# One denominator group per iteration, added up by VectorE in four pieces, with the gates kept in DRAM during attention

## The chip, the cores and the metric

The kernel runs on one core of a Trainium2 chip. The time is device microseconds of one execution; the median of three runs is the figure that is compared.

## What is computed

A transformer block with conditioning, in fp32, on x of 2 x 2048 x 512, 16 heads of 32. Cut to what matters:

```
c6 = silu(c) @ Wc + bc
sh_msa, sc_msa, g_msa, sh_mlp, sc_mlp, g_mlp = split(c6, 6)
xm = ln(x) * (1 + sc_msa) + sh_msa
q, k, v = xm @ Wq + bq, xm @ Wk + bk, xm @ Wv + bv      # 16 heads of 32
w = softmax((q / 32) @ k.T)
x = x + g_msa * ((w @ v) @ Wo + bo)
xm2 = ln(x) * (1 + sc_mlp) + sh_mlp
out = x + g_mlp * (gelu(xm2 @ W1 + b1) @ W2 + b2)
```

The softmax subtracts each row's maximum, and its denominator is the sum of the exponentials over all 2048 keys. The change is about how that denominator is made. The *gates* are g_msa, g_mlp and their products with the biases bo and b2, spread over all 128 partitions.

## The kernel before

There are three stages: `project` (0 to about 352 us), `attend` (to about 1931) and `feed_forward`. Each engine has its own program, written out by hand; engines wait for each other on semaphores, and nothing is reordered.

`attend` runs 32 iterations (2 batches x 4 groups of 4 heads x 4 blocks of 512 queries). An iteration has 16 key tiles of 128 keys, and per tile 4 heads, so 64 *slots* s. In slot s TensorE makes one score product into one of three score banks (L1058), ScalarE turns it into exponentials `probs` (L941), and TensorE makes one product for a later row maximum into one of four banks m_bank (L1042), 20 slots ahead of its use, which VectorE reduces (L963). Two tiles, 8 slots, are a *block*; blocks are numbered 0 to 7 within an iteration here. After each block's slots TensorE multiplies the previous block's probs by v (the *value group*, L1069, 16 records), and after some blocks adds up a denominator (L1075). In block 5 the row of negated maxima is made (L967, L1048, L973). The four m_bank banks are used in one fixed order, which `MaxRing` writes down: a use waits until the reader of the use four places back has finished.

The denominator of an iteration: four *quads* of four tiles. GpSimd adds probs of tiles 0 and 1 of a quad (`first_pair`, L829, in two pieces of two heads) and of tiles 2 and 3 (`second_pair`, L840, likewise), and issues DMAs that add one onto the other (`fold_quad`) and one quad onto another (`fold_half`, L844). So there are two *half sums* per iteration. TensorE multiplies each half sum by a matrix of ones, four fp32 products of one head each (`sums`, 8 records), after block 1 and block 5 (`due_sums`), as early as the fifth block behind the half sum's last. ScalarE copies the result out (`take_sum`, L888) and moves it by DMA to 128 x 16 values (`move_sums`), VectorE adds the two halves and inverts (`invert_small`, L980 and L984, at slot 3, after its maximum), ScalarE stores and reloads the inverses, GpSimd scales y (`normalise`, L859). The last iteration differs: no maxima are left, VectorE takes the first pairs (`last_first`, L1005), and the quads are summed on TensorE directly.

GpSimd's order in quad c: `first_pair` piece 0, `fold_half` if due, `fold_quad` of c - 1, `first_pair` piece 1, `normalise` in the third quad, `second_pair`. ScalarE waits before a tile's first exponential until the probs of five tiles ago are free (`slot_free`).

In `feed_forward` GpSimd adds the gate x bias to x (L1225) and VectorE multiplies the output projection by the gate (L1292); both read `sh.gates`, 16 KB in each partition, which lies in SBUF for the whole program.

## Time and profile before

| | |
|---|---|
| median of 3 runs | 2784.93 us (2783.74 to 2787.21) |
| the profiled execution | 2786.66 us, its span 2784.6 us |
| TensorE busy (PE) | 2722.4 us, 98% |
| VectorE busy (DVE) | 1990.8 us, 71% |
| GpSimd busy (POOL) | 1866.4 us, 67% |
| ScalarE busy (ACT) | 1344.0 us, 48% |

Busy shares are means over the three stages; what a change in attention is worth has to be read inside attention. In the timelines a row is one instruction or a run of equal ones (xN); the first two numbers are its start and its length in us; what stands in brackets is how long the engine had idled before it and what ended that. On GpSimd the recorded start of an instruction can lie before the end of the one ahead; the ends are what to go by.

### The profile page before, as it was taken

The page shows a single profiled execution, that of the slowest core. Times are in us where ns is not written, and L with a number is a line of the kernel's source. Part 1 is how long each engine was busy: PE and PEld are TensorE (multiplying, and loading weights), DVE is VectorE, ACT ScalarE, POOL GpSimd, SP SyncE. Part 2 cuts the span into 40 slices and gives each one's busy share as a digit, 9 for nine tenths or more (in the row PEclk, how much of TensorE's full clock was granted, in tenths as well). Part 3 has the DMA queues.
Part 4 walks back from the last instruction along what each step waited for, and adds up shares of the span by engine and source line. Part 5 has one row for each costly group of instructions (what it writes and reads, how often), then busy time and mean ns, then how long its engine had stood idle before and what let it go on. Part 6 is the DMA issues. An engine that isn't in the chain of part 4 may idle for free. (4 is left out here: it accounts for less than half of the span.)

```text
span 2784.6 us, 37794 instructions
## 1 busy us (share of the span) xinstructions
PE 2722.4 (98%) x13737; PEld 1787.1 (64%) x13737; DVE 1990.8 (71%) x3320; ACT 1344.0 (48%) x2537; POOL 1866.4 (67%) x1077
## 2 busy tenths in 40 slices
PE   7999999999999999999999999997899999999998
PEld 5777755555555555555555555542688888888887
DVE  6457688888888888888888888853666765765754
ACT  2322266676766667676676766664221221221111
POOL 1000088989899998989989899984555455455553
PEclk9999999999999999999999999998999999999999
DMA  6555468788879878887887888776000100110000
GB/s 238 192 175 177 159 133 175 165 188 175 185 168 188 183 165 186 174 187 169 188 184 167 186 175 176 154 150 221 24 28 19 46 31 16 46 42 5 31 16 16
DMA packets 143705, 369.21 MB, mean 133 GB/s; under 512 B 23524, under 2 KB 40480, under 8 KB 119712
## 3 DMA queue, kind: packets, MB, share of 16 engines
q0 software_dynamic: 26784, 195.05, 35.0%
q1 hardware_dynamic: 95388, 154.46, 18.7%
q10 hardware_dynamic: 21348, 17.28, 2.1%
q8 instruction: 110, 1.80, 0.3%
q14 instruction: 75, 0.61, 0.1%
HBM read 111.97 MB, written 58.97 MB: 61 GB/s over the span
## 5 line engine op out<-in xcount | busy, mean ns | idle before, releaser
L963 DVE TENSOR_REDUCE part_max<-m_bank 128x1 f32<-128x512 f32 x1972 | 1206.8, 679 | 275.3 <-PE m_bank L1042 275.1
L941 ACT ACTIVATE probs<-s_bank 128x512 f32<-128x512 f32 x2048 | 1034.3, 627 | 291.0 <-PE s_bank L1058 289.6
L1069 PE MATMUL y_bank<-probs,vs 128*32 128x512 f32 x4096 | 496.8, 603 | 0.0
L829 POOL TENSOR_TENSOR first_sum<-probs 128x1024 f32<-128x1024 f32 x124 | 339.2, 2736 | 87.2 <-ACT probs L941 86.8
L1425 ACT ACTIVATE h<-up_bank,vecs 128x512 f32<-128x512 f32 x128 | 88.0, 688 | 574.8 <-PE up_bank L1453 574.8
L829 POOL TENSOR_TENSOR half_sum<-probs 128x1024 f32<-128x1024 f32 x124 | 330.6, 2667 | 16.6 <-ACT probs L941 16.5
L840 POOL TENSOR_TENSOR wo<-probs 128x1024 f32<-128x1024 f32 x124 | 333.6, 3015 | 0.4 <-ACT probs L941 0.4
L840 POOL TENSOR_TENSOR second_sum<-probs 128x1024 f32<-128x1024 f32 x128 | 313.7, 2565 | 23.2 <-ACT probs L941 11.7
L1069 PEld LDWEIGHTS y_bank<-probs,vs 128*32 128x32 f32 x4096 | 107.5, 109 | 243.5 <-issue 124.4
L1058 PE MATMUL s_bank<-late_parts,keys 97*128 97x512 f32 x528 | 218.7, 418 | 1.4 <-ACT probs L941 1.4
L1331 DVE CAST h_hi<-h 128x512 fp32r<-128x512 f32 x128 | 74.4, 581 | 190.7 <-ACT h L1425 190.7
L1451 PE MATMUL up_bank<-xm_hi,w_hi 128*128 128x512 f32 x512 | 206.5, 403 | 2.8 <-DVE xm_lo L1317 2.8
L1042 PE MATMUL m_bank<-keys,late_parts 96*128 96x512 f32 x528 | 209.0, 396 | 0.0
L1239 POOL TENSOR_TENSOR w_lo<-space_plain,w_hi 128x512 fp32r<-128x512 f32 x64 | 88.0, 1376 | 179.3 <-DVE w_hi L1321 179.3
L1058 PE MATMUL s_bank<-late_parts 97*128 97x512 f32 x496 | 204.8, 414 | 0.5 <-ACT probs L941 0.5
L1453 PE MATMUL up_bank<-xm_hi,w_lo 128*128 128x512 f32 x512 | 203.5, 397 | 0.0
L1452 PE MATMUL up_bank<-xm_lo,w_hi 128*128 128x512 f32 x512 | 203.4, 397 | 0.0
L1451 PE MATMUL acc_bank<-w_hi,h_hi 128*128 128x512 f32 x512 | 202.7, 396 | 0.0
L1452 PE MATMUL acc_bank<-w_lo,h_hi 128*128 128x512 f32 x512 | 202.3, 395 | 0.0
L1453 PE MATMUL acc_bank<-w_hi,h_lo 128*128 128x512 f32 x512 | 202.2, 395 | 0.0
L1042 PE MATMUL m_bank<-late_parts 96*128 96x512 f32 x496 | 197.3, 398 | 0.9
L1239 POOL TENSOR_TENSOR w_lo<-late_plain,w_hi 128x512 fp32r<-128x512 f32 x64 | 84.1, 1314 | 169.7 <-DVE w_hi L1321 169.7
(185 smaller groups left out, 4858.6 us busy)
## 6 DMA issues: line engine op xcount, KB each, us to landing
half_sum<-second_sum POOLq DMA_DIRECT2D x62, 1024.0 KB, 13.5
first_sum<-wo POOLq DMA_DIRECT2D x62, 1024.0 KB, 9.8
half_sum<-first_sum POOLq DMA_DIRECT2D x62, 1024.0 KB, 7.4
late_plain<-in_x SPq DMA_DIRECT2D x16, 1024.0 KB, 7.4
q_parts<-qk_out SPq DMA_DIRECT2D x32, 512.0 KB, 3.5
k_parts<-qk_out SPq DMA_DIRECT2D x32, 512.0 KB, 3.4
late_parts<-q_parts SPq DMA_DIRECT2D x63, 256.0 KB, 11.5
late_parts<-k_parts SPq DMA_DIRECT2D x36, 256.0 KB, 11.4
```

The costliest lines, as they stand in the source:

```text
L829: pool.tensor_tensor(first_home(c)[:, hs, :], probs[:, 4 * c % RING, hs, :], probs[:, (4 * c + 1) % RING, hs, :], ALU.add).then_inc(first_ ...
L840: pool.tensor_tensor(second_home(c)[:, hs, :], probs[:, (4 * c + 2) % RING, hs, :], probs[:, (4 * c + 3) % RING, hs, :], ALU.add).then_inc ...
L941: act.activation(probs[:, tile % RING, h, :], s_bank[(HPG * tile + h) % 3][:, :], ACT.Exp).then_inc(p_done, 1)
L963: v.tensor_reduce(part_max[:, i % 2, hs, c:c + 1], m_bank[ring.bank["max", i, n]][:, :], AX.X, ALU.max).then_inc(m_taken, 1)
L1042: pe.matmul(m_bank[ring.bank["max", i, n]][:, :], queries[i % 3][0:STACK, h, s * P:(s + 1) * P], keys[u][0:STACK, h, :], start=True, stop= ...
L1058: pe.matmul(s_bank[n % 3][:, :], keys[u][0:STACK + 1, h, s * P:(s + 1) * P], queries[i % 3][0:STACK + 1, h, :], start=True, stop=True).the ...
L1069: last = pe.matmul(y_bank[h * DH:(h + 1) * DH, :], vs[:, t, h * DH:(h + 1) * DH], probs[:, tile % RING, h, :], start=(t == 0), stop=(t == ...
L1239: pool.tensor_tensor(w1_lo[:, j % 2, :, :], w1_raw[j * 4 // MT][:, :, j % (MT // 4) * P:(j % (MT // 4) + 1) * P], w1_hi[:, j % 2, :, :].bi ...
L1425: act.activation(h[:, j % 2, :], up_bank[j % 2][:, :], ACT.Gelu, bias=sh.vecs[:, ROW_B1 + j:ROW_B1 + j + 1]).then_inc(up_taken, 1)
L1451: pe.matmul(bank, hi_l, hi_r, start=first, stop=False)
L1452: pe.matmul(bank, hi_l, lo_r, start=False, stop=False)
L1453: return pe.matmul(bank, lo_l, hi_r, start=False, stop=last)
```

## The change

There is one denominator group per iteration instead of two. The two half sums of an iteration are added by VectorE, one head (128 x 512) at a time, `fold_whole`: two additions during the next iteration, after the maximum of slot 55 and of slot 63, and two in the one after it, after slot 7 and slot 10. TensorE then multiplies only the whole sum by ones, after block 1, so `due_sums` falls due every eighth block. The last but one iteration's two half sums are not added on VectorE; TensorE accumulates both in one bank. Three half sums in flight become five, whose SBUF comes from the gates: these are written to DRAM late in `project` and read back at the start of `feed_forward`. `invert_small` has no halves left to add and moves from slot 3 to slot 33; copying, moving, storing and reloading of the denominators move to other tiles, y is scaled an iteration later, and y_buf has three places.

```diff
+        self.gate_rows = nc.dram_tensor("gate_rows", [P, B, 4, H], F32, kind="Internal").ap()
...
                 if k == NBLK - 2:
                     sp.wait_ge(g_taken, LAST_RESULT)
                     load_early(qm[1], sh.q_parts, Q_PARTS, 1, qm_early[1])
+                    sp.dma_start(sh.gate_rows, gates[:, :, :, :]).then_inc(gates_stored, 16)
...
-    return ((b - 9) // 4,) if b >= 9 and b % 4 == 1 else ()
+    return ((b - 17) // 8,) if b >= 17 and b % 8 == 1 else ()
...
-        half_sum = [sb(f"half_sum{n}", [P, HPG, TOK]) for n in range(3)]
+        half_sum = [sb(f"half_sum{n}", [P, HPG, TOK]) for n in range(HALVES)]
...
-                if c % QPI == QPI - 2 and c // QPI >= 2:
-                    normalise(c // QPI - 2)
+                if c % QPI == 0 and c // QPI >= 3:
+                    normalise(c // QPI - 3)
+                if c == N_QUADS - 1:
+                    normalise(LAST - 2)
                 second_pair(c)
...
-                    if tile >= 20 and tile % 8 == 4 and (tile - 20) // 8 < LAST_HALF:
-                        take_sum((tile - 20) // 8)
+                    if t == 4 and i >= 2:
+                        take_sum(i - 2)
...
-            INVERT_AT = 3
+            INVERT_AT = 33
...
+            def fold_whole(i, h):
+                v.wait_ge(half_folded, 16 * (2 * i + 2))
+                onto, what = half_sum[2 * i % HALVES], half_sum[(2 * i + 1) % HALVES]
+                v.tensor_tensor(onto[:, h, :], onto[:, h, :], what[:, h, :], ALU.add).then_inc(whole_folded, 1)
+
+            FOLD_EARLY, FOLD_LATE = (55, 63), (7, 10)
...
+                    if s in FOLD_EARLY and i >= 1:
+                        fold_whole(i - 1, FOLD_EARLY.index(s))
+                    if s in FOLD_LATE and i >= 2:
+                        fold_whole(i - 2, 2 + FOLD_LATE.index(s))
                     if s == INVERT_AT and i >= 2:
                         invert_small(i - 2)
...
-                if u < LAST_HALF:
-                    pe.wait_ge(half_folded, 16 * (u + 1))
+                if u < LAST - 1:
                     for h in range(HPG):
-                        last = add_up(u, h, first_home(2 * u)[:, h, :], True, True)
+                        pe.wait_ge(whole_folded, HPG * u + h + 1)
+                        last = add_up(u, h, half_sum[2 * u % HALVES][:, h, :], True, True)
+                elif u == LAST - 1:
+                    pe.wait_ge(half_folded, 16 * (2 * u + 2))
+                    for h in range(HPG):
+                        add_up(u, h, half_sum[2 * u % HALVES][:, h, :], True, False)
+                        last = add_up(u, h, half_sum[(2 * u + 1) % HALVES][:, h, :], False, True)
...
+            sp.dma_start(gates[:, :, :, :], sh.gate_rows).then_inc(gates_in, 16)
             for c in range(4):
                 sp.dma_start(w2_raw[:, c * MT // 4:(c + 1) * MT // 4, :],
```

## Rows read from the trace of the kernel before

**Rows 1.** Busy time by stretch: length, busy us of each engine, granted clock, DMA

```profile
core 0: us, PE busy (x) PEld busy (x) DVE busy (x) ACT busy (x) POOL busy (x), PEclk, DMA share, GB/s
1000.00:1100.00 100.00, 99.83 (x562) 56.40 (x555) 80.41 (x138) 69.27 (x138) 90.67 (x48) 1.00 0.86 181
```

**Rows 2.** Timeline of TensorE, blocks 0 and 1: start, length, instruction

```profile
1040.59 0.39 PE L1042 MATMUL m_bank<-keys,space_parts 96*128 96x512 f32 x1
1040.91 1.92 PE L1069 MATMUL y_bank<-probs,vs 128*32 128x512 f32 x16
1042.76 0.50 PE L1058 MATMUL s_bank<-late_parts 97*128 97x512 f32 x1
...
1046.71 1.92 PE L1069 MATMUL y_bank<-probs,vs 128*32 128x512 f32 x16
1048.45 1.04 PE L1075 MATMUL m_bank<-half_sum,ones 128*32 128x512 f32 x8
1049.42 0.50 PE L1058 MATMUL s_bank<-late_parts,keys 97*128 97x512 f32 x1
```

**Rows 3.** Timeline of VectorE, block 7 and the next iteration's blocks 0 and 1

```profile
1031.90 4.87 DVE L963 TENSOR_REDUCE part_max<-m_bank 128x1 f32<-128x512 f32 x8 [0.93 <-PE m_bank L1042]
1037.71 2.48 DVE L963 TENSOR_REDUCE part_max<-m_bank 128x1 f32<-128x512 f32 x4 [0.94 <-PE m_bank L1042]
1040.11 0.17 DVE L980 TENSOR_REDUCE d_total<-d_small 128x16 f32<-128x32 f32 x1
...
1043.53 4.87 DVE L963 TENSOR_REDUCE part_max<-m_bank 128x1 f32<-128x512 f32 x8 [0.62 <-PE m_bank L1042]
```

**Rows 4.** Timeline of GpSimd over the same blocks, from block 6 on

```profile
1029.14 2.37 POOL L829 TENSOR_TENSOR first_sum<-probs 128x1024 f32<-128x1024 f32 x1 [0.93 <-ACT probs L941]
...
1034.97 5.35 POOL L840 TENSOR_TENSOR wo<-probs 128x1024 f32<-128x1024 f32 x2
1040.66 2.37 POOL L829 TENSOR_TENSOR half_sum<-probs 128x1024 f32<-128x1024 f32 x1 [0.34 <-ACT probs L941]
1042.97 0.90 POOL L844 DMA_DIRECT2D first_sum<-wo  x1
1043.58 2.73 POOL L829 TENSOR_TENSOR half_sum<-probs 128x1024 f32<-128x1024 f32 x1
1046.58 4.71 POOL L840 TENSOR_TENSOR second_sum<-probs 128x1024 f32<-128x1024 f32 x2 [0.26 <-ACT probs L941]
```

**Rows 5.** Timelines of VectorE, TensorE's weight loads and TensorE in block 5

```profile
1021.45 1.88 DVE L963 TENSOR_REDUCE part_max<-m_bank 128x1 f32<-128x512 f32 x3
...
1022.18 0.19 PEld L1042 LDWEIGHTS m_bank<-late_parts,space_parts 96*128 96x128 f32 x1 [0.40 <-DVE part_max L963]
...
1022.62 1.92 PE L1069 MATMUL y_bank<-probs,vs 128*32 128x512 f32 x16
```

**Rows 6.** VectorE's additions beside GpSimd's operations in the last stage; L1344 min/median/max

```profile
2077.56 4.70 DVE L1344 TENSOR_TENSOR late_plain<-late_plain 128x512 f32<-128x512 f32 x4
...
2077.39 1.42 POOL L1239 TENSOR_TENSOR w_lo<-space_plain,w_hi 128x512 fp32r<-128x512 f32 x1 [3.33 <-DVE w_hi L1321]
2078.77 1.74 POOL L1244 TENSOR_TENSOR w_lo<-w_raw,w_hi 128x512 fp32r<-128x512 f32 x1
...
L1344 DVE TENSOR_TENSOR late_plain<-late_plain x32: 677/683/1794, 2077.6 to 2781.2; 128x512 f32<-128x512 f32 x32
```

**Rows 7.** Timelines of VectorE and GpSimd, last but one iteration's end: addition beside descriptor writing

```profile
1868.68 2.54 DVE L1005 TENSOR_TENSOR half_sum<-probs 128x1024 f32<-128x1024 f32 x2 [6.35 <-ACT probs L941]
...
1869.62 0.90 POOL L844 DMA_DIRECT2D first_sum<-wo  x1 [0.62 <-POOL wo L840]
```

**Rows 8.** The sums' line: records of its matmuls on half sums

```profile
L1075 PE MATMUL m_bank<-half_sum,ones x528: 592/592/593, 414.4 to 1923.3; 128*32 128x512 f32 x176
```

**Rows 9.** GpSimd's timeline at both ends of the tail, and a stretch after it

```profile
1898.12 1.28 POOL L859 TENSOR_TENSOR y_buf<-y_buf,inv 128x512 f32<-128x512 f32 x1 [5.77 <-DMA inv<-inv_rows]
...
1938.29 6.75 POOL L1225 TENSOR_TENSOR late_plain<-late_plain,gates 128x512 f32<-128x512 f32 x4
...
1940.00:1945.00 5.00, 4.94 (x11) 2.50 (x10) 3.92 (x3) 0.00 (x0) 5.00 (x4) 0.50 1.05 396
```

## What I expect, and how I worked it out

> **What bounds the kernel now.** I read the engine table by stretch first, then the timelines of one iteration, engine by engine. In the middle of attention TensorE is busy 99.8% of the time at the full granted clock, 1.00 (the 2.4 GHz level), VectorE 80% and GpSimd 91% [rows 1]. So a microsecond taken from TensorE there comes off the end, as long as nothing makes TensorE wait. The wait that is nearest is for a maxima bank: TensorE refills bank n only when VectorE has reduced what it held four uses earlier.
>
> The iteration in the rows has take_y at 1042.9. Its blocks of two key tiles (8 scores, 8 maxima, 16 value matmuls) are 1046.71 - 1040.91 = 5.80 us long, from value group to value group [rows 2]. An iteration has eight blocks, two groups of sums and one transpose, 48.8 us in all. Inside a block VectorE is slower than TensorE: eight maxima take it 4.87 us, or 0.61 each, and it then idles 0.93 before the next block [rows 3]; TensorE issues them, a score before each, in 1046.71 - 1042.76 = 3.95 [rows 2]. The slack runs out at the eighth maximum. In block 0 it starts at 1040.59 [rows 2], and the bank it needs is freed by the fourth reduction, at 1037.71 + 2.48 = 1040.19 [rows 3].
>
> How TensorE behaves when that slack is gone stands in block 5, where the small negation delays VectorE: the reduction it waits for ends at 1021.45 + 1.88 - 2 x 0.61 = 1022.11, the weight load starts at 1022.18, the value group at 1022.62 [rows 5]. So value group = freed bank + 0.51. Undisturbed, block 0's value group starts at 1040.91 [rows 2], thus the bank may be freed as late as 1040.40: **the slack is 0.21 us**, and a delay d of the fourth reduction costs d - 0.21. A delay that comes after the fourth reduction is caught up during the value group: today's inversion sits there and the next block still starts on time [rows 2, 3].
>
> **The change, part by part.**
>
> *Fewer sums.* A value group without sums takes 1042.76 - 1040.91 = 1.85 us to the next score, with sums 1049.42 - 1046.71 = 2.71 [rows 2], so a group of sums costs 0.86. Today 62 groups of half sums run before the last iteration's own [rows 8]: 528 records of half_sum, of which 32 belong to the last iteration's quads, and (528 - 32)/8 = 62. Afterwards there are 30 single groups and one double one: 62 - 32 = 30 groups go. 30 x 0.86 = **-25.8 us**. TensorE is the bound, so it all counts.
>
> *Four additions on VectorE.* Each adds two 128x512 pieces, both in SBUF. Alone such an operation takes 0.68 and the next can start 0.61 after it (the last two of [rows 6], below). Beside a GpSimd operation it doesn't run at all until that one ends: in the last stage the four L1344 additions take 4.70 together instead of some 2.5, and the longest of all such is 1.79. The first starts at 2077.56 while a GpSimd operation runs to 2078.81; the next GpSimd operation is then itself stretched to 1.74, to 2080.51 [rows 6]. The times fit only if the first addition ran 2078.81 to 2079.35, the second ended at 2081.05, and two more took 1.2: 2077.56 + 4.70 = 2082.26. So **an addition ends 0.54 after the GpSimd operation it met**, and it gets in between two GpSimd operations that stand back to back. This agrees with the Trainium skill, "SBUF — State Buffer", section "SBUF: two separate sides": VectorE operations with two SBUF inputs and GpSimd operations take the shared port pair as an exclusive lock for a whole instruction. By the opposite view (two engines side by side) the sum would be that of the first rival below.
>
> GpSimd's pieces in attention are 2.37 us long. I walk the four additions through blocks 6, 7, 0, 1, on the clock of the rows of before. GpSimd's start in each quad is set by the exponentials, so it keeps its place against the blocks.
> - Slot 55 (end of block 6). VectorE asks at about 1030.97 (block 6's reductions start 5.80 before those of 1031.90 and last 4.87) [rows 3]. GpSimd is in the piece 1029.14 to 1031.51 [rows 4]. The addition ends 1032.05, block 7 starts 0.15 late: under 0.21, free.
> - Slot 63 (end of block 7). VectorE asks at 1036.77 [rows 3]. GpSimd's second_pair runs to 1034.97 + 5.35 = 1040.32, its second piece from 1037.95 [rows 4]. The addition ends 1037.95 + 0.54 = 1038.49; block 0's reductions start 0.78 late (1037.71). Cost 0.78 - 0.21 = **0.57**. GpSimd's second piece ends 0.54 late, 1040.86, and the next one starts 0.20 late, ending 1043.23.
> - Slot 7 (end of block 0). VectorE is done at 1038.49 + 4.87 = 1043.36, after 1043.23: GpSimd is writing descriptors. The addition is over by 1044.05; block 1, itself 0.57 late, wants VectorE at 1043.53 + 0.57 = 1044.10. Free.
> - Slot 10 (after the third of block 1). VectorE asks at 1044.10 + 3 x 0.61 = 1045.93. GpSimd's next piece ended at 1043.58 + 2.73 = 1046.31 [rows 4], now 0.20 later: 1046.51. The addition ends 1047.05, the fourth reduction 1047.70 instead of 1043.53 + 2.48 + 0.57 = 1046.58: 1.12 late, and the slack of this block is 0.19 (the value group at 1046.71 - 0.51 = 1046.20, against 1046.01): cost 1.12 - 0.19 = **0.93**.
> The maxima, and so the stalls, run in iterations 1 to 30; slot 63 hits block 0 of iterations 2 to 30, slot 10 the same 29. 29 x 1.50 = **+43.5 us**. Bounds: without any wait for GpSimd slot 10 alone costs 0.61 - 0.19 = 0.42 (12 us); with descriptor writing blocked too, the second rival.
>
> *GpSimd's own load.* It loses up to 4 x 0.54 an iteration of the 9% it idles (4.4 us) [rows 1], and waits 0.26 to 0.93 for exponentials at each start of a pair [rows 4]. The scaling of y moves from quad 2 to quad 0, ahead of a piece that today waits 0.26 for exponentials; quad 0 ends with room to spare (GpSimd is idle again before quad 1). No cost. Scalar engine loses one copy (0.6) and one DMA issue per iteration; it waits for scores anyway. Nothing.
>
> *Inversion at slot 33.* It now sits after the second reduction of block 4, but without the reduce (0.17 [rows 3]), so it delays by about 0.2: at the slack. 0, at most 0.15 x 29 = 4.
>
> *Gates through DRAM.* 2 MB out in the last block of the projection, on SP's queue ahead of eight 512 KB stores that have a ring of four buffers: hidden. Back in at the start of the last stage, ahead of W2: at the 396 GB/s of that stretch 2.1 MB take 5.3 us after a start of 2 or 3, until about 1940.5 on the old clock. GpSimd's bias additions begin at 1938.29 today [rows 9] and would slip 2; the whole four take 6.75, and TensorE works on the first products meanwhile. Nothing, at most 2.
>
> *The tail.* The move of iteration 29's sums now falls at the fifth tile of the last iteration, beside the W1 loads; the load of inverses that lies there today keeps GpSimd waiting until 1898.12, 5.77 of it idle [rows 9]. An 8 KB move that is as late would hold the scalar engine, and the exponentials of the last iteration behind it, by up to 3. I take **+1**, 0 to 4.
>
> **Sum.** -25.8 + 43.5 + 1 = +18.7. The profiled execution took 2786.7 (span 2784.6), 1.7 above the median of the runs, 2784.9. From the median: 2803.6, say **2804**.
>
> **Rivals.**
> 1. *The additions don't meet GpSimd* (its pieces shift, or the lock lets a short addition pass). Then only slot 10's own 0.42 stays: -25.8 + 12.2 = -13.6, **2771**. For it: VectorE idles 0.93 per block, more than an addition alone. Against it: the stretched rows, and that both engines' places are set by the same scores. 0.22.
> 2. *Descriptor writing is held up by the addition too.* Then slot 55 pushes GpSimd by 0.54, slot 63 ends at 1039.03 (cost 1.11), slot 7 pushes again, and slot 10 costs about 1.47: 29 x 2.58 - 25.8 = +49, **2834**. Against it here: a descriptor piece beside a VectorE addition with two SBUF inputs took 0.90 [rows 7], the same as the one at 1042.97 with no such addition beside it [rows 4]. 0.05. The Trainium skill, same page and section, describes such a hold for GpSimd-issued DMAs beside a two-port VectorE operation.
> 3. *One of the two expensive waits is not there* (slot 63 finds GpSimd between its two pieces, or slot 10 finds it writing descriptors because block 1 has slipped further). With 0.93 alone 29 x 0.93 - 25.8 = +1.2, **2787**. It decides if GpSimd's piece ends 0.6 earlier or later against the block than in the rows. 0.14.
> 4. *The forecast*, slower by 5 to 30 us: 0.59.
>
> A measurement here tells apart about 0.2%, 5.6 us. Faster 0.22, same 0.15, slower 0.63. The range, 2770 to 2818, reaches to the first rival, and upwards covers the tail, the gates, slot 33 and 0.15 us more per stall; about 0.1 lies outside on each side.
>
> **What the profile after would show.** Right: block 0 and block 1 of each iteration longer by about 0.6 and 0.9 beside others of 5.8; TensorE's weight loads for m_bank idle some 40 us on part_max; the four additions with a median over 0.8 us and a maximum near 1.9, and the sums down to half. TensorE busy in the middle nearer 97%. Wrong: additions of 0.69 throughout (first rival); stretched DMA rows on GpSimd (second); stalls in one of the two blocks only (third); the loss at the ends of attention instead of in its middle.

## The result: 3041.6 us against 2784.5, and the profile after

The changed kernel takes 3041.6 us (median of 4 runs, 3037.6 to 3044.6), the kernel before 2784.5 in the same job: a ratio of 1.092 (95% interval 1.090 to 1.093). The forecast was 2804, with a range to 2818. Its sign was right; the loss is 257 us where 19 were expected.

VectorE's additions on the page of the changed kernel, with count | busy us, mean ns of one | idle before them:

```profile
L1014 DVE TENSOR_TENSOR half_sum<-half_sum 128x512 f32<-128x512 f32 x120 | 313.1, 2611 | 0.0
```

The stretch of [rows 1] in the changed kernel, with the same columns:

```profile
1000.00:1100.00 100.00, 91.17 (x450) 46.22 (x452) 87.09 (x122) 56.66 (x110) 77.40 (x41) 0.91 0.77 160
```

An addition takes 2.61 us on average; one that meets no GpSimd operation takes 0.67. TensorE is busy 91.2 us of 100 instead of 99.8, and in that time it gets through 450 recorded matmuls where it did 562: it also runs slower, at a granted clock of 0.91 instead of 1.00. Both losses stand in the middle of attention. What it waits for is in the changed kernel's waits (engine, instruction <- what it waited for: us in total, times, longest us):

```profile
PEld m_bank L1072 <- DVE part_max L979: 146.9, 212, 2.6
...
PE m_bank L1072 <- DVE part_max L979: 121.9, 83, 2.2
```

So it is the maxima banks, as forecast; in the kernel before, TensorE's weight loads waited 15.1 us for them in all. Where the time is lost inside an iteration is read from the timelines of one iteration, VectorE first (start, length, instruction). The four additions are those of slots 55, 63, 7 and 10:

```profile
1014.71 1.07 DVE L1014 TENSOR_TENSOR half_sum<-half_sum 128x512 f32<-128x512 f32 x1
...
1020.50 4.07 DVE L1014 TENSOR_TENSOR half_sum<-half_sum 128x512 f32<-128x512 f32 x1
...
1029.28 4.84 DVE L1014 TENSOR_TENSOR half_sum<-half_sum 128x512 f32<-128x512 f32 x1
...
1035.84 0.68 DVE L1014 TENSOR_TENSOR half_sum<-half_sum 128x512 f32<-128x512 f32 x1
```

GpSimd over the same time (in brackets, the idle time before an instruction and what ended it):

```profile
1012.86 2.37 POOL L835 TENSOR_TENSOR first_sum<-probs 128x1024 f32<-128x1024 f32 x1 [1.73 <-ACT probs L954]
1015.17 0.87 POOL L854 DMA_DIRECT2D half_sum<-first_sum  x1
1015.75 1.17 POOL L854 DMA_DIRECT2D half_sum<-second_sum  x1
1016.32 3.04 POOL L835 TENSOR_TENSOR first_sum<-probs 128x1024 f32<-128x1024 f32 x1
1018.68 5.33 POOL L850 TENSOR_TENSOR wo<-probs 128x1024 f32<-128x1024 f32 x2
1026.74 2.36 POOL L835 TENSOR_TENSOR half_sum<-probs 128x1024 f32<-128x1024 f32 x1 [2.73 <-ACT probs L954]
1029.04 0.87 POOL L854 DMA_DIRECT2D first_sum<-wo  x1
1029.64 2.69 POOL L835 TENSOR_TENSOR half_sum<-probs 128x1024 f32<-128x1024 f32 x1
1032.00 1.57 POOL L869 TENSOR_TENSOR y_buf<-y_buf,inv 128x512 f32<-128x512 f32 x1
```

Read the ends. Slot 55's addition was asked for during the first piece after a pause, which ends at 1015.23, and ends at 1015.78, 0.55 later, though GpSimd's next instruction follows at once. Slot 63's was asked for at 1020.50, in the first piece of a pair; the whole pair runs to 1024.01 and the addition ends at 1024.57. Slot 7's was asked for at 1029.28, while descriptors were written; behind them stand a piece and the scaling of y, to 1033.57, and it ends at 1034.12. Each of the two waits to the end of GpSimd's row of work, and then 0.55 more. Of the 100 additions between 400 and 1850, 25 met no GpSimd operation (0.67 to 0.68), 26 met the first one after a pause and ended 0.54 to 0.56 after it, and 49 met a later one and ended 0.55 to 0.57 after the end of its whole row.

TensorE in blocks 0 and 1 of the changed kernel:

```profile
1020.74 0.50 PE L1088 MATMUL s_bank<-space_parts,late_parts 97*128 97x512 f32 x1
...
1025.22 0.50 PE L1072 MATMUL m_bank<-keys,late_parts 96*128 96x512 f32 x1 [2.10 <-DVE part_max L979]
...
1028.00 2.81 PE L1099 MATMUL y_bank<-probs,vs 128*32 128x512 f32 x16
1030.73 0.50 PE L1088 MATMUL s_bank<-space_parts,late_parts 97*128 97x512 f32 x1
...
1034.87 0.47 PE L1072 MATMUL m_bank<-keys,late_parts 96*128 96x512 f32 x1 [1.77 <-DVE part_max L979]
...
1037.90 3.64 PE L1099 MATMUL y_bank<-probs,vs 128*32 128x512 f32 x16
1041.31 1.94 PE L1105 MATMUL m_bank<-half_sum,ones 128*32 128x512 f32 x8
1043.18 0.63 PE L1088 MATMUL s_bank<-space_parts,keys 97*128 97x512 f32 x1
```

After each stall the same work is slower: the 16 value matmuls take 2.81 and 3.64 us and the sums 1.94, against 1.92 and 1.04 in [rows 2]. Counted from a block's first score, block 0 begins at 1020.74 and block 1 at 1030.73, so block 0 is 9.99 long instead of 5.80; block 1 is 1043.18 - 1030.73 = 12.45 instead of 6.66 (5.80 and one group of sums, 0.86). That is 4.2 + 5.8 - 0.86 = 9.1 us an iteration, 29 x 9.1 = 264: the whole loss (257), within 3%. The rows also part it. A value group begins 3.95 after its block's first score in [rows 2]; here it begins 1028.00 - 1020.74 = 7.26 and 1037.90 - 1030.73 = 7.17 after it, 6.5 us later in the two blocks together. The other 3.5 of the 10.0 us are the value groups and the sums themselves, which take that much longer at the lower clock.

### The profile page after: what moved, and what is told of

Same layout as the page of the kernel before. It is cut to its first block and busy times, and to the rows that moved or that the text cites. A ratio compares the mean times of both kernels' runs of the same rounds, so it can differ in the third digit from the quotient of the medians.

```text
span 3042.5 us, 37311 instructions
## 1 busy us (share of the span) xinstructions
PE 2856.3 (94%) x13497; PEld 1797.3 (59%) x13497; DVE 2279.8 (75%) x3409; ACT 1346.2 (44%) x2506; POOL 1864.1 (61%) x1077
## 3 DMA queue, kind: packets, MB, share of 16 engines
q8 instruction: 108, 1.77, 0.2%
## 5 line engine op out<-in xcount | busy, mean ns | idle before, releaser
L954 ACT ACTIVATE probs<-s_bank 128x512 f32<-128x512 f32 x2048 | 1051.0, 619 | 489.0 <-PE s_bank L1088 487.2
L1099 PE MATMUL y_bank<-probs,vs 128*32 128x512 f32 x4096 | 571.2, 682 | 0.0
L835 POOL TENSOR_TENSOR half_sum<-probs 128x1024 f32<-128x1024 f32 x124 | 314.2, 2534 | 93.7 <-ACT probs L954 93.6
L850 POOL TENSOR_TENSOR second_sum<-probs 128x1024 f32<-128x1024 f32 x126 | 297.7, 2389 | 89.8 <-ACT probs L954 89.1
L1014 DVE TENSOR_TENSOR half_sum<-half_sum 128x512 f32<-128x512 f32 x120 | 313.1, 2611 | 0.0
L1099 PEld LDWEIGHTS y_bank<-probs,vs 128*32 128x32 f32 x4096 | 117.3, 120 | 292.7 <-issue 177.9
L1072 PE MATMUL m_bank<-keys,late_parts 96*128 96x512 f32 x528 | 224.8, 426 | 45.5 <-DVE part_max L979 45.4
```

The source lines that it names most:

```text
L835: pool.tensor_tensor(first_home(c)[:, hs, :], probs[:, 4 * c % RING, hs, :], probs[:, (4 * c + 1) % RING, hs, :], ALU.add).then_inc(first_ ...
L850: pool.tensor_tensor(second_home(c)[:, hs, :], probs[:, (4 * c + 2) % RING, hs, :], probs[:, (4 * c + 3) % RING, hs, :], ALU.add).then_inc ...
L954: act.activation(probs[:, tile % RING, h, :], s_bank[(HPG * tile + h) % 3][:, :], ACT.Exp).then_inc(p_done, 1)
L1014: v.tensor_tensor(onto[:, h, :], onto[:, h, :], what[:, h, :], ALU.add).then_inc(whole_folded, 1)
L1072: pe.matmul(m_bank[ring.bank["max", i, n]][:, :], queries[i % 3][0:STACK, h, s * P:(s + 1) * P], keys[u][0:STACK, h, :], start=True, stop= ...
L1099: last = pe.matmul(y_bank[h * DH:(h + 1) * DH, :], vs[:, t, h * DH:(h + 1) * DH], probs[:, tile % RING, h, :], start=(t == 0), stop=(t == ...
```

## The experiments

Theory A (the forecast's mechanism with a new size): the time goes into the additions' waits for GpSimd and what TensorE does after them. Rivals: the gates in DRAM, the tail or the moved inversion cost it; any work of VectorE at these slots costs it. Later the question was what makes VectorE wait so long. Times are medians, ratios to the kernel before in the same job, with 95% intervals. "Additions" are the lengths of those that stand in the loop over the iterations; up to four that follow it, when no maxima are left, are not counted.

| kernel | us | ratio | additions, us |
|---|---|---|---|
| no additions | 2757.1 | 0.990 (0.988 to 0.991) | - |
| one-input reductions of the same size | 2769.3 | 0.994 (0.992 to 0.995) | - |
| slot 63 alone | 2887.3 | 1.036 (1.034 to 1.039) | 4.02 to 4.13 |
| slot 10 alone | 3028.5 | 1.087 (1.085 to 1.089) | 7.27 to 7.35, the first 1.48 |
| slot 46 alone | 2829.4 | 1.016 (1.014 to 1.018) | 1.22, or 3.97 to 5.94 |
| slot 63 alone, DMAs issued first | 2885.9 | 1.036 (1.034 to 1.039) | 1.14, or 3.5 to 5.5 |
| slots 39, 55, 7, 23 | 2932.0 | 1.053 (1.051 to 1.056) | 1.0, slot 39 mostly 5.5 to 7.5 |
| slots 55, 7, 15, 23 | 2844.3 | 1.021 (1.019 to 1.023) | 1.0 to 1.2, or 5.4 to 6.4 |
| the same, `fold_half` later | 2795.1 | 1.004 (1.002 to 1.005) | 1.0 to 1.2, seven 2.7 to 3.4 |
| the same, inversion later | **2758.5** | **0.990 (0.989 to 0.992)** | 0.94 to 1.34 |
| slot 63 alone, no DMA issues | 2878.1 | 1.033 (1.031 to 1.034) | 3.77 to 3.86 |
| four additions, no DMA issues | 2916.3 | 1.047 (1.045 to 1.049) | 0.67 to 4.28 |
| slot 63 alone, own waits | 2859.9 | 1.027 (1.025 to 1.028) | 0.68 to 2.95 |
| four additions, own waits | 2915.9 | 1.047 (1.045 to 1.048) | 0.68 to 3.37 |
| slots 55, 7, 15, 23, `fold_half` later, own waits | 2888.6 | 1.037 (1.035 to 1.038) | 0.67 to 2.49 |

### Are the additions the cause?

No additions: each one is replaced by a reduction of four elements that only signals.

```diff
-                v.tensor_tensor(onto[:, h, :], onto[:, h, :], what[:, h, :], ALU.add).then_inc(whole_folded, 1)
+                v.tensor_reduce(scrap[:, 4 * (i % 2) + h:4 * (i % 2) + h + 1], what[:, h, 0:4], AX.X, ALU.max).then_inc(whole_folded, 1)
```

> The changed kernel with the four VectorE additions of an iteration left out: in each one's place a reduction of 4 elements only signals. The denominators then hold one half sum of two, so this part of the computation is missing. Everything else of the change stays: one group of sums, gates through DRAM, the moved copies and DMAs. If all of the loss comes from the additions (theory A and B below alike): 30 groups of sums x 0.86 us = 26 us under the kernel before, 2759. If something else of the change costs (gates, tail, moved DMAs): above 2765.

The same with `what[:, h, :]`, so a reduction of 512 columns (0.61 us, an addition by itself 0.67), but with one SBUF input:

> The changed kernel with each addition replaced by a reduction over the same 128x512 piece of one half sum, at the same slots, behind the same waits. The denominators hold one half sum of two, so the addition is missing. Same length on VectorE (0.61 us each), but one SBUF input instead of two. Theory A (the additions lose because an operation with two SBUF inputs has to wait for GpSimd): each takes 0.68, only slot 10 stalls TensorE by 0.4 a time, 2759 + 12 = 2771. Theory C (it is the extra VectorE time between maxima as such, or the wait for the folded half): about the changed kernel's 3042.

Measured 2757.1 and 2769.3. The kernel without additions in the stretch from 500 to 1800 (columns of [rows 1]):

```profile
500.00:1800.00 1300.00, 1297.21 (x7192) 738.32 (x7191) 1079.28 (x1930) 904.00 (x1794) 1199.99 (x625) 1.00 0.85 180
```

TensorE is at 99.8% and full clock. Everything else of the change (gates, tail, inversion, moves) costs nothing that can be seen: 2784.9 - 25.8 would be 2759.1. Reductions of the same length cost 12.2 us more, so VectorE's time alone isn't it either. Theory A stands, both rivals fall.

### One addition at a time

Only slot 63's addition is real, or only slot 10's; the others signal as above, so the sums of the other three heads are left out.

> The changed kernel with only the addition behind slot 63 left; the other three are reductions of 4 elements that only signal, so three quarters of each denominator lack one half sum. Theory A (VectorE waits until GpSimd's whole unbroken row of pieces ends, here the two pieces of second_pair): the addition takes some 3 to 4 us, block 0 is 3 to 4 us longer, 2759 + 29 x 3 to 4 = 2846 to 2875. Theory B (as predicted: VectorE gets in between two pieces): 0.57 a time, 2776.

> The changed kernel with only the addition behind slot 10 left; the other three only signal, so three quarters of each denominator lack one half sum. Theory A: VectorE asks during the second piece of first_pair and the scaling of y follows it without a gap, so the addition takes 2.5 to 3 us and block 1 is some 2.6 us longer: 2759 + 29 x 2.6 to 3.4 = 2834 to 2858. Theory B (gets in at the end of the piece): 0.93 a time, 2786.

The additions' group in the kernel with slot 63 alone:

```profile
L1016 DVE TENSOR_TENSOR half_sum<-half_sum 128x512 f32<-128x512 f32 x30 | 121.0, 4033 | 0.0
```

Slot 10 alone, VectorE's, GpSimd's and TensorE's timelines:

```profile
1025.71 7.30 DVE L1016 TENSOR_TENSOR half_sum<-half_sum 128x512 f32<-128x512 f32 x1
...
1023.36 0.86 POOL L855 DMA_DIRECT2D first_sum<-wo  x1
1023.97 2.69 POOL L836 TENSOR_TENSOR half_sum<-probs 128x1024 f32<-128x1024 f32 x1
1026.34 1.53 POOL L870 TENSOR_TENSOR y_buf<-y_buf,inv 128x512 f32<-128x512 f32 x1
1027.57 4.88 POOL L851 TENSOR_TENSOR second_sum<-probs 128x1024 f32<-128x1024 f32 x2
...
1033.67 0.79 PE L1076 MATMUL m_bank<-keys,late_parts 96*128 96x512 f32 x1 [6.74 <-DVE part_max L980]
```

Here VectorE lets three GpSimd operations pass behind the one it met, to 1032.45, and ends at 1033.01. My expectation of this run (one more operation, at most 2858) was wrong by 170 us. One addition out of place costs 271 us (3028.5 - 2757.1); in the changed kernel slot 10 was free (0.68) only because slots 63 and 7 had already moved the block behind GpSimd's row.

### Is it the delay, or contention?

Twelve one-input reductions in slot 10's place (7.3 us of VectorE without touching GpSimd), then three and six; the others signal only.

```diff
+                for r in range(12 if h == 3 else 1):
+                    one = v.tensor_reduce(wide_scrap[...], what[:, h, :] if h == 3 else what[:, h, 0:4], AX.X, ALU.max)
+                one.then_inc(whole_folded, 1)
```

> The kernel of e4_only_slot_10 with its one addition replaced by twelve reductions over 128x512 of one half sum, one SBUF input each, 12 x 0.61 = 7.3 us; the additions are missing, the denominators hold one half sum of two. It asks whether the loss is that of VectorE's delay alone. If so (the stall of TensorE, and the granted clock that falls behind it, follow from the delay whatever makes it): the same 3028 within 10. If half the loss came from GpSimd being held or from traffic: under 2990.

> The kernel of e8 with three one-input reductions instead of twelve behind slot 10 (no additions, denominators from one half sum of two): VectorE's delay is 1.8 us, TensorE's stall 1.6. It asks from which stall on the granted clock falls. Without a fall: 2757 + 29 x 1.6 = 2804. With the full fall that twelve bring (value group 3.64 instead of 1.92, sums 1.93 instead of 1.04, 2.9 us together with the matmul before): 2888.

> The same with six: delay 3.66 us, stall 3.45. Without a fall of the clock 2757 + 29 x 3.45 = 2857; with the full one 2941.

Measured 3028.5, 2818.8 and 2896.6 (ratios 1.087, 1.012, 1.040). The twelve give exactly the time of the waiting addition (3028.5): the loss follows from the delay of VectorE's maxima, whatever makes it. It also gives the clock's price, which my sum lacked. By the forecast's rule (delay less 0.19) three, six and twelve reductions of 0.61 cost 1.64, 3.47 and 7.13 us, times 29 that is 48, 101 and 207; measured over the kernel without additions 62, 140 and 271. The difference is 0.5, 1.3 and 2.2 us an iteration, so a delay costs 1.3 to 1.4 times its length. It goes with a lower clock, 0.98, 0.97 and 0.92 on average from 500 to 1800, and with slower work after the stall: behind the twelve reductions a value group takes 3.64 us instead of 1.92.

### Where does VectorE get in?

Slot 46 stands behind the row cast, beside the quad's last pair (one addition real, as above):

> The changed kernel with only one addition left, put behind slot 46 of block 5; the other three only signal, so three quarters of each denominator lack one half sum. There VectorE asks while GpSimd is in the first of the two pieces of second_pair, which it begins after a pause for exponentials and with no descriptor writing just before. Theory A1 (VectorE is kept out only while GpSimd's records overlap, as they do behind a DMA issue; two pieces that follow without overlap leave a gap): the addition takes about 1.2 us, up to the end of the first piece, and the time is 2757 to 2762. Theory A2 (any two pieces back to back keep it out): about 3.5 us, to the end of the second piece, block 6 starts 2.4 late, and the time is 2820 to 2850.

```profile
1199.62 1.22 DVE L1016 TENSOR_TENSOR half_sum<-half_sum 128x512 f32<-128x512 f32 x1
1197.92 5.18 POOL L851 TENSOR_TENSOR second_sum<-probs 128x1024 f32<-128x1024 f32 x2
1194.74 4.17 ACT L955 ACTIVATE probs<-s_bank 128x512 f32<-128x512 f32 x8 [1.77 <-PE s_bank L1092]
...
1045.42 4.66 DVE L1016 TENSOR_TENSOR half_sum<-half_sum 128x512 f32<-128x512 f32 x1
1041.65 3.23 POOL L836 TENSOR_TENSOR half_sum<-probs 128x1024 f32<-128x1024 f32 x1
1044.02 5.49 POOL L851 TENSOR_TENSOR second_sum<-probs 128x1024 f32<-128x1024 f32 x2
1040.54 4.17 ACT L955 ACTIVATE probs<-s_bank 128x512 f32<-128x512 f32 x8 [1.76 <-PE s_bank L1092]
```

These rows are of that kernel, a short addition and a long one. In the short one GpSimd had begun the pair after a break (at 1197.92; the piece before it had ended at 1197.78), and VectorE got in between the pair's two pieces; in the long one the pair followed the piece before without one. Half of the additions, 14 of 28 up to 1850, were short, so the measured 2829.4 lies in the range of theory A2 only as a mixture of both kinds. What the pair's second piece needed had been there 0.71 us before VectorE asked both times (ScalarE's exponentials end at 1198.91 and 1044.71): its data being ready is not what tells the two apart. The next kernel issues the DMAs ahead of `first_pair`, with slot 63 alone:

> The kernel of e3_only_slot_63 (one addition, behind slot 63; the others only signal, three quarters of each denominator lack one half sum) with GpSimd's DMA issues moved ahead of first_pair, to where it then pauses for exponentials, so that no descriptor writing stands just before its pieces. Theory A1: the addition ends behind the piece it met, 1 us or so, 2757 to 2775. Theory A2: it waits for both pieces of second_pair, some 3.5 us, and the time is about 2840 or more, near e3's 2887.

The lengths alternated: about 1.14 where the pair had begun after a pause (and once where the records show none), 3.5 to 5.5 where not. The time, 2885.9, is that of slot 63 alone, but not for the same reason: moving the issues has a cost of its own. From 500 to 1800 VectorE waited 45.0 us in 13 waits, up to 12.0 each, for the small sums' DMA ahead of the inversion, and TensorE's longest stall, 11.6 us, is for the maxima behind it. So this time says nothing on the additions; their lengths do.

Then two complete kernels that move all four additions (and, for the buffers, the sums from block 1 to block 3, the copies and stores of denominators a quad later, the inversion to slot 51 and the scaling of y to the third quad):

```diff
-            FOLD_EARLY, FOLD_LATE = (55, 63), (7, 10)
+            FOLD_EARLY, FOLD_LATE = (39, 55), (7, 23)      # first kernel
+            FOLD_EARLY, FOLD_LATE = (55,), (7, 15, 23)     # second kernel
```

> The whole computation, with the four additions behind slots 39, 55, 7 and 23, the ends of even blocks, where VectorE asks during GpSimd's first piece of a quad, after which it writes descriptors; sums after block 3, copies and DMAs of the denominators four tiles later, inversion behind slot 51, scaling of y in the third quad. Theory A (both kinds): each addition ends 0.55 behind that first piece, takes 1.0 to 1.1 and delays the next block by 0.1 to 0.15, below the slack of 0.21: no stall, 2757 to 2764, 25 under the kernel before. If descriptor writing keeps VectorE out as well: each takes over 5 us, above 3000.

> The whole computation: the kernel of e7 with slot 39 given up; the additions stand behind slots 55, 7, 15 and 23. At each of these GpSimd is in a piece that it began after a pause (55, 7, 23: the first of a quad; 15: the first piece of second_pair in the first quad), and by theory A1 VectorE gets in behind that one piece. Expected: all additions 1.0 to 1.1 us, no stall over 0.1, the full gain of the 30 groups of sums: 2758 to 2764. If two pieces in a row keep VectorE out whatever went before (A2), those behind slot 15 take over 3 us and the time is 2830 or more.

2932.0 and 2844.3. In the second, slots 7, 15 and 23 were 1.0 to 1.2 almost everywhere; slot 55 took 5.4 to 6.4 in 12 of the 28 iterations up to 1850. GpSimd had waited for a fold's DMA to land (52.1 us in all, in 23 waits); where that wait was 2.3 us or longer, it had no pause ahead of the quad of slot 55, and the addition was long, and where it was 2.2 or less, the addition was short. So `fold_half` is issued one piece later:

```diff
-                if c % 2 == 1 and 3 <= c <= LAST_QUAD + 1:
-                    fold_half((c - 3) // 2)
                 if 1 <= c <= LAST_QUAD:
                     fold_quad(c - 1)
                 if c < LAST_QUAD:
                     first_pair(c, PAIR[1])
+                if c % 2 == 1 and 3 <= c <= LAST_QUAD + 1:
+                    fold_half((c - 3) // 2)
```

> The whole computation: the kernel of e9 with GpSimd's issue of fold_half moved behind the second piece of first_pair, 2.4 us later in the quad, so that it needn't wait for the landing of the quad's DMA before it (3.3 and 2.5 us in e9, 21 times), which took GpSimd's pause ahead of the next two quads away. Theory A1: with the pause back, the additions behind slot 55 (in e9 1.0 or 5.4 to 6.4 us) are all near 1.0, as those behind 7, 15 and 23 are, and nothing stalls: 2758 to 2768. If the long ones have another cause than the lost pause: as e9, 2844.

2795.1. Its seven longer additions, one of them, by VectorE, GpSimd and TensorE:

```profile
682.45 0.25 DVE L1002 RECIPROCAL inv_small<-d_small 128x16 f32<-128x16 f32 x1 [1.26 <-DMA d_small<-d_raw]
...
684.96 2.85 DVE L1018 TENSOR_TENSOR half_sum<-half_sum 128x512 f32<-128x512 f32 x1
...
681.66 2.37 POOL L837 TENSOR_TENSOR first_sum<-probs 128x1024 f32<-128x1024 f32 x1 [0.46 <-ACT probs L956]
683.97 0.88 POOL L856 DMA_DIRECT2D half_sum<-second_sum  x1
684.58 2.67 POOL L837 TENSOR_TENSOR first_sum<-probs 128x1024 f32<-128x1024 f32 x1
686.90 1.18 POOL L856 DMA_DIRECT2D half_sum<-first_sum  x1
...
688.55 0.77 PE L1077 MATMUL m_bank<-space_parts,late_parts 96*128 96x512 f32 x1 [2.51 <-DVE part_max L983]
```

VectorE had waited 1.26 us for the inversion's data (0.73 to 1.40 in the seven), asked late, and met the next piece. It got in at that piece's end (687.25; the addition ends at 687.81), ahead of a DMA issue that itself has to wait for the fold issued at 683.97.

### What closes the gap?

In attention every long row held descriptor writing; in [rows 6] there is none. Two kernels replace each fold's DMA by a short GpSimd addition (256 columns of one head only; the rest of the folds is left out):

```diff
-                return pool.dma_start(onto.rearrange("p h n -> p (h n)"), what.rearrange("p h n -> p (h n)"), accum_op=ALU.add)
+                return pool.tensor_tensor(onto[:, 0, 0:256], onto[:, 0, 0:256], what[:, 0, 0:256], ALU.add)
```

> As the kernel with the addition of slot 63 alone, but every DMA that GpSimd issues for the folds is replaced by one short addition of GpSimd (256 elements wide, about 0.6 us, the distance between two descriptor records), so GpSimd's rows are as dense as before and hold no descriptor writing. It leaves out the folds' sums but for those 256 columns, so the denominators are not right. Theory D (descriptor writing is what closes the gap between two pieces): VectorE asks while the first piece of second_pair runs and gets in behind it, additions of 1.2 to 2.0 us, time 2765 to 2795. Theory R (any piece that was already issued and waits for nothing closes the gap, descriptor writing or not): additions of 3.5 to 4.2 us as in the kernel with slot 63 alone (4.03), time 2870 to 2900.

> The changed kernel with all four additions on VectorE, and GpSimd's DMAs for the folds replaced by its own short additions as in the kernel with slot 63 alone (the folds' sums are left out but for 256 columns). Theory D: the four additions take 0.7 to 2.0 us each, time 2770 to 2820. Theory R: slots 63 and 7, or others in their place, 3.5 to 7 us long, time 2950 to 3060.

The first, GpSimd and VectorE:

```profile
1021.14 2.40 POOL L836 TENSOR_TENSOR first_sum<-probs 128x1024 f32<-128x1024 f32 x1
1023.50 4.80 POOL L851 TENSOR_TENSOR wo<-probs 128x1024 f32<-128x1024 f32 x2
...
1025.09 3.77 DVE L1016 TENSOR_TENSOR half_sum<-half_sum 128x512 f32<-128x512 f32 x1
```

No descriptor is written, and VectorE still passes over the boundary inside the pair and ends at 1028.86, 0.56 after it. So descriptor writing isn't needed to close the gap. The second run fits neither theory's number (2916): slot 63 stayed at 4.21 to 4.28, but slot 7 fell to 0.67 to 1.21, where the changed kernel has 4.84. Mostly it met the short addition that stands behind the first piece without a pause, and got in behind that one. So a pause before the operation it meets isn't the only way in.

The last theory, Q: VectorE is held behind those operations that GpSimd has already been given. To open every gap GpSimd waits for its own operation before:

```diff
+                own(c)      # wait_ge on first_ready, second_ready and y_normed for all that GpSimd has issued
                 pool.tensor_tensor(first_home(c)[:, hs, :], probs[:, 4 * c % RING, hs, :],
```

(and so ahead of each of its operations and DMA issues in attention).

> As the kernel with the addition of slot 63 alone (whole sums left out but for that piece), with one thing more: ahead of every operation of its own in attention GpSimd waits for the semaphore of its operation before it. So it can't be given an operation while the one before still runs; the work and its order are the same, DMA issues included. Theory Q (VectorE is held behind those GpSimd operations that had been given to the engine ahead): VectorE asks while the first piece of second_pair runs and gets in behind that piece, additions of 1.2 to 2.0 us instead of 4.03, time 2765 to 2795. Theory R (any GpSimd row without a pause holds VectorE to its end): additions of 3.8 to 4.3 us, time 2880 to 2900.

> The changed kernel, complete, with GpSimd's waits for its own operation before. Theory Q: the additions end about 0.55 us after the one GpSimd piece they met and are 0.7 to 3 us long; that is what the forecast assumed, so the time should come near it, 2785 to 2830. Theory R: as the changed kernel, additions of 4 to 5 us at slots 63 and 7, time 3020 to 3060.

> The kernel with the additions behind GpSimd's pauses and fold_half issued later (2795), with GpSimd's waits for its own operation before. Theory Q: the seven or eight additions of some 2.8 us at slot 55 fall to under 1.5 or so, the rest stay 1.0 to 1.2, time 2770 to 2790. Theory R: no change in the long ones, 2790 to 2800.

Slot 63 alone with own waits, GpSimd and VectorE:

```profile
1016.68 2.94 POOL L847 TENSOR_TENSOR first_sum<-probs 128x1024 f32<-128x1024 f32 x1
1019.84 2.65 POOL L864 TENSOR_TENSOR wo<-probs 128x1024 f32<-128x1024 f32 x1 [0.22 <-issue]
...
1018.88 1.30 DVE L1033 TENSOR_TENSOR half_sum<-half_sum 128x512 f32<-128x512 f32 x1
```

The piece ends at 1019.62, the addition at 1020.18, and GpSimd's next piece is stretched to 2.65: the forecast's picture of a gap. In the changed kernel with own waits, up to 1850, 104 of the 106 additions that met a GpSimd operation end about 0.55 after that very one, and none takes over 3.4; without own waits, 49 of the 75 that met one waited for the row's end. This shows that VectorE gets in behind nearly every single operation when GpSimd waits for its own end before the next. It doesn't show Q's reason: each own wait also puts a pause, 0.22 us here and 0.68 ahead of a DMA issue, behind every operation, and no run has the one without the other.

The times missed all three expectations (2859.9, 2915.9, and 2888.6 for the kernel that took 2795.1), and their waits from 500 to 1800 say why. First the changed kernel with own waits, then slots 55, 7, 15, 23:

```profile
PE m_bank L1089 <- DVE part_max L996: 66.7, 64, 2.8
PE s_bank L1110 <- ACT probs L973: 71.6, 122, 0.8
```

With the additions in their old places TensorE still waits for the maxima, since an addition takes up to 3.37 us. With the additions behind the pauses it waits for exponentials instead, and ScalarE waits 110.8 us in all (132 waits) for GpSimd's additions to free probs, which it never does in the last kernel below: GpSimd, 91% busy in [rows 1], with its own waits on top sets the pace there. TensorE is busy 1228 us of 1300, at a clock of 1.00.

The last run acts on the reading of the seven longer additions instead, without own waits: the inversion goes behind slot 55's addition.

```diff
-            INVERT_AT = 51
+            INVERT_AT = 59
...
-                        if t == (13 if i < LAST else 9):
+                        if t == (15 if i < LAST else 9):
                             store_inv(i - 2)
```

> The kernel with the additions behind GpSimd's pauses and fold_half issued later (2795), complete, with one more step: the inversion of the small sums at slot 59 instead of 51, after slot 55's addition, and its store two tiles later. Its trace had seven iterations in which VectorE waited 1.26 us for the sums' DMA ahead of that inversion, came late to slot 55's addition, met GpSimd's second piece instead of the one after the pause (2.7 to 3.4 us instead of 0.98) and made TensorE stall 2.5 us; the other iterations kept TensorE at 99.8% and 1.00. Theory Q (held behind what GpSimd was given ahead; a late request is what costs): no addition over 1.3 us, TensorE 99.8% throughout, time 2762 to 2774, faster than the kernel before. If these long additions have another cause: 2790 to 2800 as it was.

Its stretch from 500 to 1800, and then GpSimd's and VectorE's timelines around slot 55:

```profile
500.00:1800.00 1300.00, 1297.39 (x7191) 736.90 (x7190) 1173.41 (x1928) 905.41 (x1794) 1215.74 (x625) 1.00 0.85 181
```

```profile
1018.18 2.37 POOL L837 TENSOR_TENSOR first_sum<-probs 128x1024 f32<-128x1024 f32 x1 [0.60 <-ACT probs L956]
1020.49 0.87 POOL L856 DMA_DIRECT2D half_sum<-second_sum  x1
...
1020.02 1.08 DVE L1018 TENSOR_TENSOR half_sum<-half_sum 128x512 f32<-128x512 f32 x1
```

2758.5, a ratio of 0.990 (0.989 to 0.992): 4 us below the expected range and 26 below the kernel before, with the whole sum computed. TensorE is back at 99.8% and 1.00. All 116 additions in the loop take 0.94 to 1.34; each meets the first piece after a pause. Four more follow the loop, from 1826, and take up to 8.88, when VectorE has no maxima left to delay. Four additions an iteration that cost 284 us in the changed kernel over one without them cost 1.4 at these slots, which is within the measurement.

## Why the prediction was wrong

1. *The sums*, -25.8: right. Without the additions the change gives 2757.1, and 2758.5 with additions that are free.
2. *Gates, tail, inversion, GpSimd's load*, +1: right within the measurement (2757.1 against 2759.1).
3. *An addition's own length*. Slot 10's bound without any wait for GpSimd was 12 us; the one-input reductions cost 12.2.
4. *The slack of 0.21 and the banks as the place of the wait*: right: blocks 0 and 1 are the long ones, the weight loads and matmuls wait on part_max, and the slack fits the 12.2 us of step 3.
5. *"It gets in between two GpSimd operations that stand back to back"*: **this step failed.** The end, 0.54 after the GpSimd operation, was right to 0.02 us, but the operation is often not the one it met. Slot 63 waited to the end of the pair (4.07 instead of the walk's 1.72, 1038.49 - 1036.77), slot 7, which I had free, 4.84. I had read the rule from a single case, [rows 6], where GpSimd had waited 3.33 us before the operation that VectorE met; by the runs a pause like that lets VectorE in, and I carried the rule to rows without one, where it mostly has to wait on. The Trainium skill ("SBUF — State Buffer", section "SBUF: two separate sides") says beside the lock that "There are deep queues that would have to be drained to share"; I weighed only its lock for one instruction. Here the measurement differs from a lock that ends with the instruction: VectorE waited through two pieces (4.07 us) and through four operations (7.30). The sentence on the queues fits that, but gives no condition for a gap.
6. *The clock*: a term that the sum put at nothing without a reason; it priced a stall at its length. In the iteration shown, 3.5 of 10.0 us are slower work. By the reductions a delay of 3.5 us costs 4.8, one of 7.1 costs 9.4.
7. *GpSimd's place*: that its start "is set by the exponentials, so it keeps its place against the blocks" was wrong too. Ahead of the quads that begin in blocks 6 and 0 GpSimd pauses 1.73 and 2.73 us for exponentials in the changed kernel, where [rows 4] have 0.93 and 0.34; the delayed scores would do that, which no run tests by itself. Slots 7 and 10 changed parts: the one I had free took 4.84, the one I priced at 0.93 was free.

Of the rivals, the second had the larger loss (2834) but the wrong mechanism: descriptor rows are no longer than before (0.87 us against 0.90), and the run with no descriptor writing shows long waits all the same. Of what I named as signs, the median over 0.8 and the longer blocks came; "a maximum near 1.9" and "TensorE busy in the middle nearer 97%" were not met (the mean alone is 2.61, and TensorE is at 91.2%). That the sign was right is no success of the walk: its sum of the two stalls, 1.50 us an iteration, is under a sixth of the 9.8 that the additions cost (284 us in 29).

What stays open is why VectorE gets in behind the first operation after a pause even though the next one follows at once (26 of 26 in the changed kernel, 116 of 116 in the last), while later in a row it is mostly held. Over the eleven kernels that have real additions and no own waits, up to 1812 us, all 482 additions that met an operation begun after a pause of 0.13 us or more got in behind it. Of the 256 that met one without such a pause 210 were held beyond it, 17 met the last of a row, and 29 got in all the same, 16 of these behind the short additions that stand in the place of the DMA issues. That VectorE is held behind what GpSimd was given ahead would fit the own waits and the late `fold_half`, but it is argued, not shown: the data of the next piece were ready before the request in short and long waits alike, and what GpSimd had been given by then was not measured.

## What to carry to other kernels

Before putting a two-input VectorE operation into a loop where GpSimd works, find in GpSimd's timeline the instruction it will meet and ask whether a pause stands before it: if so it costs about one microsecond, if not, mostly the rest of GpSimd's row. Place such operations behind GpSimd's pauses, and take every wait for a DMA off both engines ahead of that spot, since a request that is 1.3 us late meets another piece. Where the bound is TensorE, price a delay of some microseconds above its length (1.3 to 1.4 times here, at one delay an iteration), and don't take a rule on contention from one row without looking at what stood before it.

## What the runs showed of the hardware

- A VectorE addition with two SBUF inputs that meets GpSimd ends about 0.55 us after GpSimd's operation or row of operations, whether its wait was 0.4 us (length 1.08) or 6.6 (7.30).
- After a GpSimd pause, even one of 0.13 us, it got in behind the first operation every time (482 of 482).
- In a GpSimd row without a pause it is mostly held, for instance through three operations behind the one that it met (7.30 us in all). One-input reductions of the same size in its place cost next to nothing (2769.3 against 3041.6).
- It is also held where GpSimd writes no descriptors (3.77 to 3.86 us), and it gets in where GpSimd waits for its own operation before (104 of 106), at 0.22 us of idle time each.
- After stalls of TensorE of 2.10 us, and of 1.77 and 0.47, value groups took 2.81 and 3.64 instead of 1.92 us. The granted clock of the stretch was 0.91 on average, between the full level (2.4 GHz, 1.00) and the lower one (1.2 GHz).
